# Modulated rows made inside the first layer's loop instead of in a prologue

## The reference, cut to what matters

```python
mod = (silu(c) @ wmod).reshape(8, 6, 1, 512)
sa, ca, ga, sb, cb, gb = (mod[:, k] for k in range(6))
# ga and gb: sign kept, magnitude at least 0.25
h = layernorm(x) * (1 + ca) + sa            # x: 8 sequences x 1024 tokens x 512
for i in range(2):                          # two layers
    res = h
    h = layernorm(h, ln_w[i], ln_b[i])
    h = mamba2(h, ...)                      # project, conv, scan over tokens, gate, RMS norm, project
    h = h + res
x = x + ga * h
h = layernorm(x) * (1 + cb) + sb
x = x + gb * channel_mix(h)
```

## Time and profile before

| what | value |
|---|---|
| time, median of 3 runs | 4278.69 us |
| profiled execution: its own time | 4276.1 us |
| profiled execution: its span | 4274.3 us |
| TensorE matmul busy | 4005.1 us (94%) |
| VectorE busy | 3465.9 us (81%) |
| ScalarE busy | 2899.9 us (68%) |
| GpSimd busy | 2026.9 us (47%) |

### The profile page before, as it was taken

How to read it: one execution, slowest core, us unless ns; L and a number is a source line. 1 busy time by engine, 2 the same in 40 slices (tenths; PEclk the granted TensorE clock), 3 DMA queues, 4 the chain that set the end, 5 groups by cost and what they waited for, 6 DMA issues and landing times. The chain is left out here.

```text
span 4274.3 us, 100194 instructions
## 1 busy us (share of the span) xinstructions
PE 4005.1 (94%) x38872; PEld 3600.5 (84%) x38872; DVE 3465.9 (81%) x5227; ACT 2899.9 (68%) x4898; POOL 2026.9 (47%) x1572
## 2 busy tenths in 40 slices
PE   4599999999999999969999999999999996799999
PEld 1599999899999999958999999999999995577777
DVE  8688888888888888868888888888888885666664
ACT  4577777677777777747777777777777773666664
POOL 7344444444444444424444444444444444566664
PEclk6799999999999999979999999999999998899999
DMA  8400000000000000020000000000100002222220
GB/s 327 142 31 31 31 31 31 31 31 31 31 31 31 31 33 32 26 96 29 31 31 31 31 31 31 31 33 35 37 31 31 31 26 85 82 97 97 85 83 33
DMA packets 115764, 220.03 MB, mean 51 GB/s; under 512 B 10792, under 2 KB 20520, under 8 KB 114472
## 3 DMA queue, kind: packets, MB, share of 16 engines
q1 hardware_dynamic: 115376, 214.25, 14.1%
HBM read 146.97 MB, written 67.24 MB: 50 GB/s over the span
## 5 line engine op out<-in xcount | busy, mean ns | idle before, releaser
L508 PE MATMUL l_ring<-l_u_hi,l_wi_lo 128*128 128x256 f32 x4608 | 1318.2, 286 | 22.2 <-ACT l_raw L754 12.4
L508 PE MATMUL l_ring<-l_u_lo,l_wi_hi 128*128 128x256 f32 x4608 | 1296.6, 281 | 0.0
L508 PE MATMUL l_ring<-l_u_hi,l_wi_hi 128*128 128x256 f32 x4608 | 1296.0, 281 | 0.0
L1008 DVE SCALAR_TENSOR_TENSOR l_xc<-l_raw,l_prm,l_xc 128x256 f32<-128x256 f32 x1536 | 958.3, 668 | 96.4 <-ACT l_xc L763 78.2
L508 PEld LDWEIGHTS l_ring<-l_u_hi,l_wi_lo 128*128 128x128 f32 x4608 | 873.1, 189 | 48.3 <-issue 16.9
L508 PEld LDWEIGHTS l_ring<-l_u_lo,l_wi_hi 128*128 128x128 f32 x4608 | 874.0, 190 | 11.7
L1199 POOL TENSOR_TENSOR l_g<-l_g 128x512 f32<-128x512 f32 (+2 forms) x384 | 355.6, 926 | 1096.1 <-ACT l_g L824 1076.0
L508 PEld LDWEIGHTS l_ring<-l_u_hi,l_wi_hi 128*128 128x128 f32 x4608 | 873.9, 190 | 0.0
L1170 POOL TENSOR_TENSOR l_rhs<-l_cum,l_small 32x1024 fp32r<-32x1024 f32 x256 | 497.5, 1952 | 154.1 <-PE l_wide L570 103.8
L1190 POOL TENSOR_TENSOR l_g<-l_g,l_zs 128x1024 f32<-128x1024 f32 x128 | 306.0, 2391 | 449.9 <-DVE l_g L1055 448.5
L508 PE MATMUL l_ring<-l_wo_hi,l_g_lo 128*128 128x512 f32 x1024 | 414.0, 404 | 18.9 <-DVE l_g_lo L1060 11.3
(11 more groups left out here) (168 smaller groups left out, 8060.3 us busy)
## 6 DMA issues: line engine op xcount, KB each, us to landing
l_hn<-h_scratch SPq DMA_DIRECT2D x64, 512.0 KB, 3.8
l_res<-h_scratch SPq DMA_DIRECT2D x128, 256.0 KB, 3.6
h_scratch<-l_res SPq DMA_DIRECT2D x128, 256.0 KB, 2.1
m_rows<-in_x SPq DMA_DIRECT2D x16, 1024.0 KB, 9.3
h_scratch<-m_rows SPq DMA_DIRECT2D x16, 1024.0 KB, 7.0
f_x<-in_x SPq DMA_DIRECT2D x16, 1024.0 KB, 5.6
f_h<-h_scratch SPq DMA_DIRECT2D x16, 1024.0 KB, 8.0
out<-f_x SPq DMA_DIRECT2D x64, 256.0 KB, 2.0
```

What stands on the lines that cost most here:

```text
L508: last = nc.tensor.matmul(out, a, c, start=(k == 0), stop=(k == n - 1))
L1008: ins = nc.vector.scalar_tensor_tensor(out=acc, in0=raw[:, (s + c) % 2, k, tap:tap + TB], scalar=prm_sb[:, w:w + 1], in1=acc, op0=ALU.mult ...
```

## The change

`prologue` becomes `modulation`, which makes the six terms, stores them to DRAM and touches no rows. Layer 0 now loads rows of `x`. For each segment there are, on the tile `hn`: `raw_stats` (VectorE), `raw_inv_std` and `raw_offset` (GpSimd), `raw_normalise` (ScalarE), `modulate` (GpSimd: two multiplications by the scale row, two additions of the shift row), and `keep` (SyncE), which stores the modulated rows to `h0`, from where they are loaded as the residual. Then the layer's own statistics and `normalise` follow as before, `normalise` behind the store. Scale and shift row share one tile `mod_row`, broadcast from DRAM: the shift row is loaded once the multiplications are through, the next scale row once the additions are.

The order of layer 0's segment changes too: `sum_parts` stands ahead of `low_g(b, s, 0)`, the second statistics behind `stationary_sums`, `normalise` between taps 2 and 3, and GpSimd's `inv_std` between the next segment's two `moving`. In both layers `res` becomes one buffer for both halves: the second half's residual is loaded after the first half's result is stored. Layer 1 keeps its order otherwise.

```diff
-def prologue(nc, sems, x, h, cT, wmod, cst, mod_dram, cols_dram, nseq):
+def modulation(nc, sems, cT, wmod, cst, mod_dram, cols_dram, nseq):
+    order = (2, 5, 3, 4, 0, 1)
...
+            for k, n in enumerate(order):
+                sp.dma_start(w_sb[:, n], wmod[:, :, n * DM:(n + 1) * DM]).then_inc(s_w[k], 16)
...
+            sp.wait_ge(s_term, 6)
+            sp.dma_start(mod_dram.rearrange("b (s d) -> b s d", s=6), mod_sb[:]).then_inc(s_kept, 16)
+            sp.wait_ge(s_cols, 1)
+            sp.dma_start(cols_dram.rearrange("b p k -> p b k"), cols_sb[:]).then_inc(s_kept, 16)
...
-        res = sb("res", [P, NPAIR, DM])
+        res = sb("res", [P, DM])
+        mod_row = sb("mod_row", [P, DM])
...
+            def keep(b, s):
+                i = NB * b + s
+                kept = src[bass.ds(i * TB, TB), :]
+                sp.wait_ge(s_add, NPAIR * (i + 1))
+                sp.dma_start(kept.rearrange("(t p) d -> p t d", p=P), hn[:]
+                             ).then_inc(s_kept, 16)
...
             load(b0, 0)
+            if first:
+                load_row(0, 0, mod_row[:])
+                load_row(0, 1, first_shift)
...
                 row = (i - NB * b0) * TB
-                for j in range(NPAIR):
-                    sp.wait_ge(s_store[j], 16 * i)
-                    sp.dma_start(res[:, j], src[bass.ds(row + j * P, P), :]
-                                 ).then_inc(s_res[j], 16)
-                for j in range(NPAIR):
-                    sp.wait_ge(s_out, NPAIR * i + j + 1)
-                    sp.dma_start(dst[bass.ds(row + j * P, P), :], res[:, j]).then_inc(s_store[j], 16)
+                sp.wait_ge(s_store[1], 16 * i)
+                sp.dma_start(res[:], src[bass.ds(row, P), :]).then_inc(s_res[0], 16)
+                if first and n2:
+                    nxt2, nxt3 = ahead(b, s, 2), ahead(b, s, 3)
+                    sp.wait_ge(s_mul, NPAIR * (i + 3))
+                    load_row(nxt2[0], 1, mod_row[:])
+                    keep(*nxt2)
+                    if not (isinstance(b, int) and b == nseq - 1 and s == NB - 3):
+                        load_row(nxt3[0], 0, mod_row[:])
+                sp.wait_ge(s_out, NPAIR * i + 1)
+                sp.dma_start(dst[bass.ds(row, P), :], res[:]).then_inc(s_store[0], 16)
+                sp.wait_ge(s_store[0], 16 * (i + 1))
+                sp.dma_start(res[:], src[bass.ds(row + P, P), :]).then_inc(s_res[1], 16)
+                sp.wait_ge(s_out, NPAIR * i + 2)
+                sp.dma_start(dst[bass.ds(row + P, P), :], res[:]).then_inc(s_store[1], 16)
...
                 new_state(b, s, 0, 1)
+                if first and n2:
+                    raw_normalise(*ahead(b, s, 2))
                 decays(b, s, 1, 0)
...
+            if first:
+                raw_normalise(0, 0)
             for n in range(2):
                 split_high(n)
...
             conv_in(b0, 0, 2, 2)
+            if first:
+                raw_normalise(0, 1)
             silu_x(b0, 0, 1)
...
             def normalise(b, s):
+                if first:
+                    dve.wait_ge(s_kept, 16 * (NB * b + s + 1))
                 dve.wait_ge(s_rstd, NB * b + s + 1)
...
                 matrices(b, s, 0, 0)
+                if first and n2:
+                    raw_stats(*nxt2)
                 if n1:
                     steps(*nxt)
...
                 matrices(b, s, 1, 0)
+                if first and n1:
+                    sum_parts(*nxt)
                 low_g(b, s, 0)
-                if n2:
+                if n2 and not first:
                     row_stats(*nxt2)
                 if n1:
-                    sum_parts(*nxt)
+                    if not first:
+                        sum_parts(*nxt)
                     taps(*nxt, 1)
                 y_read(b, s, 1, 0)
                 matrices(b, s, 1, 1)
                 if n1:
                     stationary_sums(*nxt)
                 if n2:
-                    normalise(*nxt2)
+                    if first:
+                        row_stats(*nxt2)
+                    else:
+                        normalise(*nxt2)
                 mean_square(b, s, 0)
...
                 finish(b, s, 0)
                 if n1:
                     taps(*nxt, 2)
+                if first and n2:
+                    normalise(*nxt2)
+                if n1:
                     taps(*nxt, 3)
...
+            def modulate(b, s, scale_row, shift_row, rows):
+                m = NB * b + s
+                scale_loaded, shift_loaded = rows
+                pool.wait_ge(s_row, scale_loaded)
+                for t in range(NPAIR):
+                    pool.wait_ge(s_xnorm, NPAIR * m + t + 1)
+                    nc.gpsimd.tensor_tensor(hn[:, t, :], hn[:, t, :], scale_row, ALU.mult).then_inc(s_mul, 1)
+                pool.wait_ge(s_row, shift_loaded)
+                for t in range(NPAIR):
+                    pool.wait_ge(s_mul, NPAIR * m + t + 1)
+                    nc.gpsimd.tensor_tensor(hn[:, t, :], hn[:, t, :], shift_row, ALU.add).then_inc(s_add, 1)
...
                 skip_term(b, s, 1)
+                if first and n2:
+                    raw_inv_std(*nxt2)
+                    raw_offset(*nxt2)
                 gate(b, s, 0)
+                if first and n2:
+                    i = NB * b + s
+                    modulate(*nxt2, mod_row[:], mod_row[:], (32 * (i + 1), 32 * (i + 1) + 16))
                 squares(b, s, 0)
-                if n2:
+                if n2 and not first:
                     inv_std(*nxt2)
                 if n1:
                     moving(*nxt, 0)
+                if n2 and first:
+                    inv_std(*nxt2)
+                if n1:
                     moving(*nxt, 1)
                 inv_rms(b, s, 0)
```

## The result

The changed kernel takes 4360.28 us (median of 4 runs, 4354.22 to 4361.73), against 4278.08 us for the kernel before on the same chip (4 runs): a ratio of 1.019, 95% interval 1.0176 to 1.0204. It is 82 us slower; 35 us slower were forecast, and the range ended at 4345. The direction was right, the size was not.

A forecast was written before the change was run, and what follows sets the result against it. TensorE bounds the kernel, running its list without gaps, tied to VectorE at `low_g(b, s, 1)`. 4276.1 - 97.4 (prologue) + 20.8 (opening) + 111 (30 segments) = 4310, 4313 us by the median, +0.8%; range 4226 to 4345.

The forecast's parts named there:

- Prologue and opening: Before layer 0's loop: prologue keeps only modulation terms, -97.4 us; the first two segments' longer path costs 20.8 us.
- Hidden pieces: Layer 0 segments: raw statistics, ScalarE's two steps (1.5 us), sums' split and the store fit idle time, costing nothing.
- The single residual buffer: Both layers: second residual load waits for the first store, 6.5 us, hidden with 9 us to spare.
- rival B: Layer 0 segments: the shift row lands late, at 6 us; 2.2 us a segment, 66 us, total 4268; chance 0.11.
- The sixth ends at 1070.1: VectorE's taps in layer 0: five GpSimd operations let five taps through, the sixth ends at 1070.1; 0.6 us gain left.
- `finish` 2.7 us late, `normalise` 1.0: Layer 0 segment: `finish(b, s, 0)` starts 2.7 us late, `normalise` adds 1.0, so `low_g(b, s, 1)` ends 3.7 us late.
- 30 x 3.7 = 111 us: Layer 0's loop: TensorE loses 3.7 us in each of 30 segments, 111 us in all; ends 27 and 141 us.
- A: Layer 0 segments: GpSimd's additions and second statistics are hidden, only `normalise`'s 27 us stay; 4229 by the median; chance 0.28.
- C: Opening and loop: upper ends together, 4.7 us a segment and an opening of 30 us; 4350; chance 0.11.

The follow-up runs named there:

- small additions: Changed kernel with the shift row added to only 8 of 512 columns (shift left out of 504): 4226.46 us, 0.9884 of the kernel before.
- early row: Changed kernel with the shift row loaded at the segment's head into `g_lo`'s first half, additions directly after multiplications: 4241.82 us, 0.9912 of before.
- filling the waits: Changed kernel with 16 and 14 unread identity transposes added on TensorE ahead of its two waits in layer 0: 4321.45 us, 1.0102 of before.
- the early row and `inv_std` later: Kernel with the shift row loaded at the segment's head, plus GpSimd's `inv_std` behind both `moving` and `inv_rms`: 4224.48 us, 0.9877 of before.
- `inv_std` later: Changed kernel with GpSimd's `inv_std` moved behind both `moving` and behind `inv_rms(b, s, 0)`: 4298.04 us, 1.0053 of before.
- `normalise` last: `normalise` moved behind `low_g(b, s, 1)`, in the kernel with the early row and `inv_std` later: 4248.01 us, 0.9934 of before.

## Why the prediction was right in direction and wrong in size

- **Prologue and opening: right.** -97.7 for -97.4, +19.6 for +20.8. The stages' marks show the sums, not each of their parts.
- **Hidden pieces: right.** Raw statistics (1.28 us and the aggregates) end at 1048.5, before L887 at 1048.60; ScalarE's two steps take 1.52 us where it still waited 0.39 us afterwards. The single residual buffer costs nothing (experiment). GpSimd stood idle 98.3 us in 30 times for the shift row, 3.3 us each, where 3.5 was forecast; rival B did not occur. (B's own sum is off by little: `finish` at 1077.8 is 1.4 us late and not 1.2.)
- **"The sixth ends at 1070.1": wrong, by a term.** Five taps were let through one by one, as forecast: single taps began at 1065.27, 1066.70, 1068.24, 1069.56 and 1070.55. But the sixth was not free (VectorE's timeline, a narrow window):

```profile
1071.04 2.12 DVE L931 SCALAR_TENSOR_TENSOR l_xc<-l_raw,l_prm,l_xc 128x256 f32<-128x256 f32 x1
```

  Right behind the squares GpSimd begins its first `moving` at 1070.81, for 2.08 us, and the tap ended 0.27 us after it. I had counted the GpSimd operations up to the squares and stopped. The taps took 7.89 us where the forecast had 6.2. (Its own terms, 1063.8 + 2.6 + 2.9, end at 1069.3 and not 1069.6; that goes the other way.)
- **"`finish` 2.7 us late, `normalise` 1.0": right in mechanism, slightly low.** Measured against TensorE's own list, `finish` ends 2.27 us after TensorE came to projection 7; before, it ended 1.25 us ahead of it (1077.19 and 1078.44). It is 3.5 us late in this segment. The longer taps add 1.7; the taps' start, some 0.6 us earlier than forecast in the same measure, takes part of it back. With `normalise`, TensorE loses 2.27 + 1.91 = 4.2 us in this segment and 3.86 on the mean of 30. That the late taps are the root, the small additions and the early row show. `inv_std`'s place passes their delay on (moved behind, it takes the wait at projection 7 from 64.0 to 3.8 us), and it costs some 0.7 us a segment even with the row early.
- **"30 x 3.7 = 111 us": the step that failed.** The waits measured 115.7 us. The loop lost 157.8. The term that the sum lacked is TensorE's granted clock after most pairs of waits, 42 us in all, 1.4 a segment; filling the waits gave 39 us back and left the chain on the other engines as it was. The waits themselves were 4.7 us over the sum. Of the 51 us between the forecast for the profiled execution, 4310, and its 4361.73, the loop holds 46.8 and the unexplained stop in layer 1 most of the rest. I had weighed the slower clock for the opening and for the modulation block, and took the loop's matmuls at their old durations while I gave TensorE two new pauses.
- **Rivals.** A asked whether additions beside taps are free. They are not. Its number, 4229, with only `normalise`'s 27 us left, is what the kernel takes when they are out of the way and `inv_std` is in time: 4226 with small additions, 4224 with the early row and `inv_std` later. C came nearest in time (4350), with 4.7 us a segment and a bad opening; the opening was not bad, and the loop lost 5.3 a segment, so its nearness is luck.

## What to carry to other kernels

When a change gives a full TensorE a new wait, price the wait and then what its matmuls do afterwards: here 116 us of waits of about 2 us drew 42 us of slower clock after them, while the kernels with one wait of 1.0 or 1.7 us a segment kept 1.00. Work put on GpSimd beside a chain of VectorE instructions is priced by listing every GpSimd operation up to the end of that chain, those that were there already included, since the added delay pushes the chain into them. And a transfer that must land between two GpSimd steps decides what the second step collides with: giving it a buffer of its own was worth 118 us here.

## What the runs showed of the hardware

- The clock drop is short and repeated: two pauses of TensorE of about 2 us, 9 us apart, and then 0.69 and 0.74 over 3 us each. With one pause of 2.3 us a segment (`inv_std` later) or one of 1.8 us (`normalise` last) the loop's mean is 0.99, with one of 1.7 us (row early) 1.00.
- Two `tensor_scalar` steps of VectorE, with a single SBUF tensor, were held by GpSimd as well: the sums' split took 1.27 us in place of 0.35 (early row), and the two stationary sums, 0.35 us alone, took 1.57 beside `moving` (small additions). `bn_stats` was not: 1.28 us for two beside GpSimd (small additions), 1.29 with GpSimd idle (changed kernel). The Trainium skill (SBUF — State Buffer, Who interferes with whom) names `tensor_scalar` among the operations that can take the shared port pair; the rows agree.
- Two GpSimd additions of 8 columns (0.85 us for both) held the taps almost not at all: six in 2.71 us, the first beginning 0.3 us after the additions did.
